# Two loops of a slot-routing kernel reordered on VectorE: the routing weights and the last layernorm

## What is computed

```python
x = x + layernorm(cumulative_mean(layernorm(x)))   # first half
z = layernorm(x)                                   # second half
h = gelu(concat(z, slot_mean) @ w1 + b1)           # 4096 x 512
L = (h @ w2 + b2) / (abs(tau) + 0.1)               # 4096 x 64 slots
alpha = softmax over the 8 largest of each row, 0 elsewhere
si = (alpha.T @ z) / alpha.sum(0)                  # 64 x 1024
S_new = GRU(si, slot_init); slots attend to slots; layernorm; two projections
x = x + layernorm(alpha @ slot_values @ wo + bo)
```

## Time and profile before

| | us |
|---|---|
| timed, median of 2 runs | 1008.86 (1004.45 to 1013.26) |
| the profiled execution | 984.39 |
| its span on the slowest core | 982.8 |
| spans of the 8 cores | 956.5 to 982.8 |
| alpha loop, about | 603 to 686 |
| last loop, about | 842 to 976 |

### The profile page before, as it was taken

How to read it: one execution, slowest core, us unless ns; L and a number is a source line. 1 busy time by engine, 2 the same in 40 slices (tenths; PEclk the granted TensorE clock), 3 DMA queues, 4 the chain that set the end, 5 groups by cost and what they waited for, 6 DMA issues and landing times.

```text
span 982.8 us, 8916 instructions; the slowest of 8 cores (956.5 to 982.8 us)
## 1 busy us (share of the span) xinstructions
PE 413.6 (42%) x2605; PEld 192.4 (20%) x2610; DVE 308.9 (31%) x1056; ACT 255.8 (26%) x330; POOL 145.9 (15%) x83
## 2 busy tenths in 40 slices
PE   0014244533544200778888885444121356322220
PEld 0000000000000000566666663121121111000000
DVE  0023445254335588011100113444201010455552
ACT  0003332424242300323222324565000110133332
POOL 2003132312332300000000001000000000043434
PEclk9999555555555555587855787555555556555555
DMA  7998999999500010011111110000452313023234
GB/s 193 267 289 116 110 107 107 107 125 108 68 0 0 6 27 0 2 33 33 33 33 33 33 33 2 1 1 5 106 115 57 101 47 106 22 101 156 108 148 171
DMA packets 69294, 76.40 MB, mean 78 GB/s; under 512 B 53216, under 2 KB 57312, under 8 KB 68640
## 3 DMA queue, kind: packets, MB, share of 16 engines
q0 software_dynamic: 4800, 22.25, 20.0%
q1 hardware_dynamic: 64448, 53.60, 18.2%
HBM read 68.72 MB, written 36.70 MB: 107 GB/s over the span
## 4 chain that ended last, share of the span: by engine, by line
PE 34%; DVE 28%; issue 11%; ACT 10%; DMA 8%; another core or an unknown queue 7%; DVEq 1%; ACTq 1%; POOLq 0%; POOL 0%; SPq 0%
DVE bn6x L192 12%; PE p_h L541 10%; DVE bn6c L192 4%; DMA whhT<-wih_bf 4%; PE pcs L386 3%; PE p_f L1078 3%; PE pcs L394 3%; PE p_h L545 2%; ACT fnb L207 2%; ACT anb L207 2%; PE p_xt L531 2%; PE ptot L398 2%; ACT x3b L207 2%; DVE x3t L195 2%
## 5 line engine op out<-in xcount | busy, mean ns | idle before, releaser
L541 PE MATMUL p_h<-x3t,sb_w1a 128*128 128x128 bf16 x1024 | 106.2, 267 | 37.7 <-DVE x3t L195 24.6
L412 POOL TENSOR_TENSOR sb_x<-anb,sb_x 128x1024 f32<-128x1024 f32 x32 | 75.6, 2380 | 181.7 <-ACT anb L207 181.7
L386 PE MATMUL pcs<-x1b,s_tri 128*128 128x512 bf16 x60 | 31.2, 617 | 145.2 <-ACT anb L207 140.1
L541 PEld LDWEIGHTS p_h<-x3t,sb_w1a 128*128 128x128 bf16 x1024 | 78.8, 119 | 52.5 <-issue 43.6
L192 DVE BATCH_NORM_STATS2 bn6c<-pcs 128x6 f32<-128x512 f32 x64 | 39.9, 685 | 134.0 <-PE pcs L394 128.7
L195 DVE COPY x3t<-p_xt 128x1024 bf16<-128x1024 bf16 x32 | 22.1, 692 | 181.3 <-PE p_xt L531 181.3
L192 DVE BATCH_NORM_STATS2 bn6x<-sb_x 128x6 f32<-128x512 f32 x128 | 77.5, 678 | 0.0
L207 ACT ACTIVATE stat<-stat 128x2 f32<-128x2 f32 (+1 forms) x64 | 13.0, 203 | 224.6 <-DVE stat L184 223.1
L1140 POOL TENSOR_TENSOR sb_x<-fnb,sb_x 128x1024 f32<-128x1024 f32 x24 | 55.8, 2338 | 97.8 <-ACT fnb L207 97.8
L1078 PE MATMUL p_f<-sb_sv,sb_alphaT 64*128 64x512 bf16 x64 | 31.8, 609 | 88.4 <-ACT fnb L207 86.0
L192 DVE BATCH_NORM_STATS2 bn6x<-p_f 128x6 f32<-128x512 f32 x64 | 39.9, 686 | 64.4 <-PE p_f L1078 64.4
(11 more groups left out here) (174 smaller groups left out, 527.3 us busy)
## 6 DMA issues: line engine op xcount, KB each, us to landing
sb_x<-x SPq DMA_DIRECT2D x8, 2048.0 KB, 38.3
out<-sb_x SPq DMA_DIRECT2D x8, 2048.0 KB, 6.8
whh_bf<-Whh POOLq DMA_DIRECT2D x1, 6144.0 KB, 60.9
wih_bf<-Wih POOLq DMA_DIRECT2D x1, 6144.0 KB, 118.1
wv_bf<-wv POOLq DMA_DIRECT2D x1, 2048.0 KB, 145.6
wvp_bf<-wvp POOLq DMA_DIRECT2D x1, 2048.0 KB, 163.4
wo_bf<-wo POOLq DMA_DIRECT2D x1, 2048.0 KB, 178.6
wst<-wv_bf SPq DMA_DIRECT2D x8, 256.0 KB, 2.6
```

Of the source, the lines that this page charges most:

```text
L386: ins = t.matmul(b[:, h * DH:(h + 1) * DH], c_tri[:], x1t[:, h * DH:(h + 1) * DH], start=True, stop=(j == 0))
L412: g.tensor_tensor(sb_x[:, j * D:(j + 1) * D], anb[:, (j % 2) * D:(j % 2 + 1) * D], sb_x[:, j * D:(j + 1) * D], op=OP.add).then_inc(sX2, 1)
L541: t.matmul(ph[:, jc * P:(jc + 1) * P], w1av[:, dc, jc * P:(jc + 1) * P], x3tv[:, dc * P:(dc + 1) * P], start=(jc == 0 and dc == 0), stop=F ...
```

## The change

Two loops on VectorE are put in another order; no operation is added or removed.

In the alpha loop the body is split. The second part (`altail`) of tile j-1 runs after the first part (`m8`, `eb`) of tile j. `m8b` and `zcol` get two halves, chosen by j % 2, and `m8` j now also waits for `exp` j-2, which read the half that it overwrites. ScalarE reads the half of its tile.

In the last loop, `p5tail(pr-1)` and, for even `pr`, `vadd` come before the wait for TensorE and the statistics of pair `pr`; before, they came after them.

```diff
-        m8b = sb2b("m8b", [P, 8])
+        m8b = sb2b("m8b", [P, 16])
-        zcol = sb2b("zcol", [P, 4])
+        zcol = sb2b("zcol", [P, 8])
...
-            for j in range(NT):
-                v.wait_ge(sSSG, V(("lg", j // 8), 0))
+            def altail(j):
                 lt = sb_L[:, j * NS:(j + 1) * NS]
-                val["m8", j] = VMX(m8b[:], lt)
-                val["eb", j] = VTT(zcol[:, 1:2], m8b[:, 0:1], sb_ninv[:], OP.mult)
                 v.wait_ge(sSSG, V(("exp", j), 0))
                 ev_ = sb_E[:, (j % 2) * NS:(j % 2 + 1) * NS]
                 au = aub[:, (j % 2) * NS:(j % 2 + 1) * NS]
-                val["au", j] = VSTT(au, lt, m8b[:, 7:8], ev_, OP.is_ge, OP.mult, accum=zcol[:, 0:1])
-                VRC(zcol[:, 2:3], zcol[:, 0:1])
+                val["au", j] = VSTT(au, lt, m8b[:, (j % 2) * 8 + 7:(j % 2) * 8 + 8], ev_,
+                                    OP.is_ge, OP.mult, accum=zcol[:, (j % 2) * 4:(j % 2) * 4 + 1])
+                VRC(zcol[:, (j % 2) * 4 + 2:(j % 2) * 4 + 3], zcol[:, (j % 2) * 4:(j % 2) * 4 + 1])
                 if j >= 2:
                     v.wait_ge(sP3T, j - 1)
-                val["alf", j] = VTS(sb_alpha[:, j * NS:(j + 1) * NS], au, zcol[:, 2:3], None, OP.mult)
+                val["alf", j] = VTS(sb_alpha[:, j * NS:(j + 1) * NS], au,
+                                    zcol[:, (j % 2) * 4 + 2:(j % 2) * 4 + 3], None, OP.mult)
                 if j % 4 == 3:
                     v.wait_ge(sP3T, j + 1)
                     val["ate", j // 4] = VCP(sb_alphaT[:, (j - 3) * P:(j + 1) * P], p_at[0:NS, :])
+
+            for j in range(NT):
+                v.wait_ge(sSSG, V(("lg", j // 8), 0))
+                if j >= 2:
+                    v.wait_ge(sSSG, V(("exp", j - 2), 0))
+                val["m8", j] = VMX(m8b[:, (j % 2) * 8:(j % 2) * 8 + 8], sb_L[:, j * NS:(j + 1) * NS])
+                val["eb", j] = VTT(zcol[:, (j % 2) * 4 + 1:(j % 2) * 4 + 2],
+                                   m8b[:, (j % 2) * 8:(j % 2) * 8 + 1], sb_ninv[:], OP.mult)
+                if j >= 1:
+                    altail(j - 1)
+            altail(NT - 1)
...
-                                     bias=zcol[:, 1:2], scale=sb_invt[:])
+                                     bias=zcol[:, (j % 2) * 4 + 1:(j % 2) * 4 + 2],
+                                     scale=sb_invt[:])
...
                 for pr in range(NPAIR):
+                    if pr >= 1:
+                        p5tail(pr - 1)
+                    if pr >= 2 and pr % 2 == 0:
+                        vadd(4 * ((pr - 2) // 2) + 1)
                     v.wait_ge(sCS, NT + 2 * pr + 2)
                     for j in (2 * pr, 2 * pr + 1):
                         VBN(bn6x[:, j * 12:j * 12 + 6], p_f[j % 4][:, 0:DH])
                         val["bn5", pr] = VBN(bn6x[:, j * 12 + 6:j * 12 + 12], p_f[j % 4][:, DH:D])
                     val["c5", pr] = combine(SM_MX, SM_VX, bn6x, 2 * pr, 2, None)
-                    if pr >= 1:
-                        p5tail(pr - 1)
-                    if pr >= 2 and pr % 2 == 0:
-                        vadd(4 * ((pr - 2) // 2) + 1)
                 p5tail(NPAIR - 1)
                 vadd(NT - 3)
```

## The result

| | before | after |
|---|---|---|
| timed, median | 992.39 us (980.63 to 1013.26, 10 runs) | 950.80 us (941.55 to 972.57, 11 runs) |
| ratio of medians of comparable runs | | 0.9589, interval 0.9527 to 0.9651 |
| profiled execution | 984.39 | 958.63 |

The change makes the kernel 4.1% faster, 41.6 us between the medians.

A forecast was written before the change was run, and what follows sets the result against it. No engine is full in either loop; both were taken as bound by rings of hand-overs between engines. Savings of 23.8 (alpha loop) and 14 (last loop), 37.8 us, off 1008.9 gave 971 us, range 952 to 988.

The forecast's parts named there:

- the last one of the sum: Whole kernel: the 37.8 us saving taken off the 1008.9 us median of two timed runs, giving 971 us.
- Stage A: Alpha loop: last alf at 660.2 us against 684.0, 23.8 us saved, bounds 19 to 26.
- Rival 5: Alpha loop: PE's clock rises to 2.4 GHz, shortening the loop by 4 us more, 967 us; chance 0.04.
- Rival 3: Alpha loop gains half, 12 us, because ACT's in-order queue closes a ring, 983 us; chance 0.11.
- the walk: Alpha loop: one group of four tiles followed in time, 7.3 us for 10.2, x2b waiting for PE two tiles back.
- Stage B: Last loop: pairs of 6.0 and 8.25 us in turn for 8.03, 14 us saved, bounds 0 to 39.
- the term of the odd pair: Last loop: combination product t0 waits out both POOL additions (8.3 us) or slips between them (8.15); 8.25 taken.
- first F: Last loop: F is the start of ACT's first fn of a pair; the first was put at 849.4 us.
- stray stalls: Last loop: stalls of a few tenths expected to recur, so 14 us saved taken instead of 14.6.
- Rival 1: Last loop: POOL does not hold DVE's operations, 39 us saved there, 946 us in all; chance 0.09.
- Rival 2: Last loop gains nothing: odd pairs wait out each addition, an even pair's operation is caught twice; 985 us, chance 0.12.
- rival 4: Last loop: POOL's additions keep DVE out altogether, statistics and vadd too; loses 38 us, 1023 us; chance 0.03.

The follow-up runs named there:

- steady base: Kernel before and changed kernel, both with TensorE's logits of tile j-1 moved ahead of the wait for tile j's copy: 951.83 and 912.66 us.
- early logits: Changed kernel, GELU stage: TensorE does tile j-1's logits between tile j's transposes and the wait for their copy: 907.35 us; on the kernel before, 951.83.
- late copy: Changed kernel with the alpha loop's copy of the four transposes put three tiles later, from two PSUM buffers: 944.32 us.
- thin additions: Changed kernel with POOL adding only 64 of 1024 columns of its tiles in the last loop: 931.04 us.
- two and two: Changed kernel with the last loop's additions split evenly, DVE adding odd tiles and POOL even ones: 934.68 us.

## Why the prediction was right in its steps and wrong in its number

**What failed is the base.** The step that failed is the last one of the sum, "the saving is the same number of microseconds there: 971". The saving was put at 37.8 us; the measurements give 41.6 (all runs), 40.6 (one session) and 39.2 (steady base). The number, 971, stood on the median of two timed runs, 1008.86, which the text itself found 24 us above the profiled execution and could not explain. Ten runs have 992.39 as the median, and 992.4 - 37.8 = 954.6, 0.4% from 950.8. Of the 20 us between 971 and 950.8 the base makes 16.5 and the saving 3.8. The range, 952 to 988, was made from the rivals alone; the base had an uncertainty from 984 to 1009, as large as most of the rivals, and no term for it. The low end missed by 1.2 us.

The base's scatter comes from the stage ahead of the alpha loop, the GELU stage, which the change doesn't touch. Cores 2 and 6 of the kernel before in the table of stretches (the row of core 2 first; the granted PE clock is the third column from the right):

```profile
392.00:560.00 168.00, 135.91 (x1348) 102.62 (x1349) 17.86 (x29) 46.03 (x54) 0.00 (x0) 0.66 0.12 28
392.00:560.00 168.00, 132.70 (x1619) 100.97 (x1619) 20.76 (x30) 52.49 (x62) 0.00 (x0) 0.88 0.15 34
```

and the first and last `alf` of core 6; those of core 2 stand in the earlier trace rows, 605.2 to 684.0:

```profile
L178 DVE TENSOR_SCALAR sb_alpha<-aub,zcol x32: 253/254/255, 576.6 to 655.4; 128x64 bf16<-128x64 f32 x32
```

At a mean granted clock of 0.66 the stage ends 28.6 us later than at 0.88, and the alpha loop behind it is 78.8 us on both. From the first `x3b` to the first `alf` the stage took 186.0 to 211.9 us on the eight cores, while no other stretch from there on differs by more than 7 us, and the spans of the cores go with it (correlation 0.98). The time is that of the slowest core, in both profiled runs the one whose clock in this stage was lowest. The early logits put some 0.5 us of matmuls a tile into TensorE's wait of 1.2, and with them the four runs of the kernel before spread over 2.2 us instead of 23 over seven; the mean clock of 392 to 560 us is then 0.83 to 0.96 over the cores, where the kernels without them have 0.66 to 0.88 (before) and 0.55 to 0.91 (changed). Over all kept traces the stage takes 181 to 235 us without the early logits and 161 to 180 with them. That a smaller hole and a higher clock go together is shown by this experiment; why the chip grants the one or the other on a given core is not. That the two timed runs in the base were high for this reason is likely but not shown, since no trace of them was kept.

**Stage A.** Said: 55.0 us from first to last `alf`, 23.8 saved. Measured: 54.1 to 56.4, in the mean 55.4. The group was walked at 7.3 us, and this one on core 0 takes 7.34:

```profile
615.39 0.42 DVE L195 COPY sb_alphaT<-p_at 64x512 bf16<-64x512 bf16 x1 [1.64 <-PE p_at L664]
622.73 0.41 DVE L195 COPY sb_alphaT<-p_at 64x512 bf16<-64x512 bf16 x1 [1.55 <-PE p_at L664]
```

The seven groups of core 0 run from 6.75 to 7.69 and average 7.29, so that the agreement to a hundredth is luck. Rival 5, given 4 in 100, came true in part. On core 2 the clock rises inside the loop (mean 0.62 for 0.50 in the earlier trace rows), PE's pair of matmuls takes 0.59 us instead of 1.03 (at 621.97), and four of its seven groups take 6.8 to 7.0:

```profile
588.00:643.00 55.00, 34.69 (x125) 15.88 (x126) 33.13 (x193) 45.23 (x64) 1.30 (x2) 0.62 0.04 1
```

Its price, 0.5 us a group, was right, and its effect is 1 to 2 us. Rival 3 is out: `x2b`'s wait for PE stands in the walk and costs what it did there, 2.8 us in all on core 2. The experiment with the late copy shows what was left: the wait for the transposes held a group at 7 us, without it a group takes 5.7 (44.2 us over 31 steps).

**Stage B.** Said: pairs of 6.0 and 8.25, 14 us saved. Measured: 6.0 and 7.94, 16.3 alone. The mechanism was right, the term of the odd pair mis-sized by 0.3: of its two forms (8.3 if t0 waits out both additions, 8.15 if it slips between them) the second happened in six pairs of seven, and I had POOL's second addition pushed back by the slip. It is not: the two take 4.64 us as before (818.05 to 822.69), and the caught product is free 0.2 us sooner. In the seventh pair t0 was held, and the pair lasted 8.30. Together the seven take 56.0 us for the 57.75 of the sum, 1.8 less. The earlier first F, put at 3 us (849.4 for 852.3), gave 2 to 5 in the means over the cores, and the 0.6 held back for stray stalls was not needed, since the loop before had its own (two of its steps of 8.03 are 8.38). Rival 1 is out by the thin additions, whose steps, 4.85 and 6.00, are close to the 4.86 and 6.08 that the prediction gave for a loop free of POOL. Rival 2 is out by the loop's 105.0 us for 118.6, rival 4 by bn_stats, 2.49 us for four beside the additions (817.64).

**The sum.** 22.1 + 16.3 = 38.4 by the medians, against the 37.8 predicted. By the profiled runs of the two kernels, in the mean over the cores: the alpha loop went from 78.8 to 55.4 us, the stretch from the last `alf` to the first `fn` from 170.4 to 166.5, the last loop from 118.7 to 105.1. That is 23.4 + 3.9 + 13.6 = 40.9 us. So stage A was put 0.4 too high and stage B, at 14, 3.5 too low. What stands behind the last `fn` is as long as before, 12.0 us.

## What to carry to other kernels

When two queues hand work to and fro, put the next item's first half ahead of this item's second half, and walk one group from the trace's own start-to-start times: here that gave both loops within 2 us of their length. After such a move look at what a small DVE operation now runs beside: here POOL's additions, which read SBUF, held the DVE operations with two SBUF inputs that came under them to their end, and bn_aggr in the place of such operations took 29 us more out of the last loop, an even split of the additions 13.5, where the move had taken 13.6. And before a time is predicted, find the stage whose length differs between the cores of one run; its spread belongs in the range, whatever the change touches.

## What was not expected of the hardware

- A DVE product that comes between two back-to-back POOL additions gets through (820.32, 0.16 us) and doesn't delay the second (4.64 us for both). The one that came 0.24 us after the start of the second was held (890.33, 2.12 us).
- A held product ends 0.01 to 0.05 us after POOL's addition (822.70 against 822.69, 828.37 against 828.34).
- An addition of 1024 columns is held too: DVE's last addition of the kernel with two and two, at 920.09 on core 0, took 2.37 us instead of 1.23 beside POOL's, which ended at 921.37.
- The GELU stage's mean granted clock ran from 0.55 to 0.91 (392 to 560 us) over the cores of the profiled runs of the kernel before and the changed one. Moving five small matmuls a tile into TensorE's wait, 0.5 us of its 1.2, took 43 us off the kernel (34 in the mean over the cores), more than the 11 that a shorter tile gives at an unchanged clock.
